# Attention value matmuls: three key tiles of four in two fp16 parts, and half of the mask made by GpSimd

## The chip, the cores and the metric

One core of one Trainium2 chip. The metric is the device time of one execution in microseconds, median of several runs; a profiled execution of the same kernel gives the trace.

## The reference, cut to what matters

Four layers run one after the other on 4096 nodes with 128 features: graph attention, a mixture of experts, a second graph layer, a second mixture. The change is in the first, and in the mask that the third reads:

```python
Qn = _cos_normalize(features @ Wq.T)
Kn = _cos_normalize(features @ Wk.T)
raw_att = Kn @ Qn.T
att = jnp.where(adj > 0, raw_att, NEG) * TEMP
att = jax.nn.softmax(att, axis=1)
prop_fea = att @ features
...
mask = (adj[:M] > 0) & valid[None, :]
```

`adj` is 4096 x 4096 int32, 64 MB. The scores are cosines, so the softmax needs no maximum: exp(score), times (adj > 0), summed over the keys.

## The kernel before, in words

`prepare` normalizes the rows, keeps them as values for attention and makes the queries' and keys' unit vectors, each as a high and a low fp16 part. It works in 8 groups of 512 nodes. Its `low_values` on GpSimd copies the fp32 values (L204) and subtracts the high fp16 part (L206), which ScalarE made in `high_values` (L283).

`attend` has 128 steps. Step k is (c, jp): c is one of 8 groups of 512 nodes that receive, jp one of 16 pairs of 128-row key tiles. All engines run their own unrolled list and meet by semaphores:

- SyncE loads 512 KB of adjacency (int32, 128 x 1024) into a ring of 4 buffers (L391). A buffer is free once the mask multiplication has read it.
- TensorE runs `scores(k + 2)`, six fp16 matmuls of 128x512 (L411), then `gather(k)`: the values times the probabilities, summed in one PSUM bank over the 16 pairs. The first key tile of a pair is one fp32 matmul (L423), the second is three fp16 ones: low values x high probabilities (L425), high x high (L426), high values x low probabilities (L428).
- ScalarE runs `exponentials(k + 1)` (L461), `keep_high(k)`, the copy of the second tile to fp16 (L469), and `keep_mask(k)`, the Sign of both tiles as uint8 (L472), which stays in SBUF for the third layer.
- VectorE runs `mask_exponentials(k + 1)` (L488: probs = (adj > 0) x probs), then `keep_low(k)` (L494: probs - p_hi), then, at jp 0, 3, 5 and 7, a piece of the `ending` of the previous group c: L507 copies the sums, L511 to L517 prepare, L524 adds, L532 measures.
- GpSimd has no work in this stage.

At jp 1 TensorE also turns the previous group's sums back (L437, four matmuls, eight records). The waits: L411 of k + 2 waits for the exponentials of k to have read their banks; L423 for the masked probabilities; L425 for p_hi, L428 for p_lo. The buffers p_hi and p_lo are two deep, probs four.

Of the kernel before, what the change touches and what calls it, by code (L numbers as in the profile page):

```python
# [7 lines left out]
F32 = mybir.dt.float32  # L8
# [9 lines left out]
P = 128  # L18
# [13 lines left out]
SLOTS = 2  # L32
LEVEL = 60.0
# [81 lines left out]
def prepare(nc, io, sb, ps):  # L115

    with ExitStack() as ctx:
# [18 lines left out]
        pairs = lambda ap: ap.rearrange("p (a b) d -> p a b d", b=2)  # L136
# [32 lines left out]
        with nc.Block() as block:  # L169
# [15 lines left out]
            @block.gpsimd  # L185
            def _(pool):
                nc.gpsimd.memset(sb["ident"][:, :], 0.0).then_inc(ident_ready, 1)
                pool.wait_ge(ident_ready, 1)
                nc.gpsimd.affine_select(out=sb["ident"][:, :], in_=sb["ident"][:, :], compare_op=ALU.not_equal,
                                        fill=1.0, base=0, pattern=[[-1, P]], channel_multiplier=1).then_inc(ident_ready, 1)  # L190
                nc.gpsimd.memset(v32[:, :, D - 1:D], V_SCALE).then_inc(ident_ready, 1)
                nc.gpsimd.memset(v16[:, :, 0, D - 1:D], V_SCALE).then_inc(ident_ready, 1)
                nc.gpsimd.memset(v16[:, :, 1, D - 1:D], 0.0).then_inc(ident_ready, 1)
                nc.gpsimd.memset(sb["turn"][:, :], 0.0).then_inc(ident_ready, 1)
                pool.wait_ge(ident_ready, 6)
                nc.gpsimd.tensor_copy(sb["turn"][:, 0:D - 1], sb["ident"][:, 0:D - 1]).then_inc(ident_ready, 1)
                nc.gpsimd.tensor_copy(sb["turn"][:, D:D + 1], sb["ident"][:, D - 1:D]).then_inc(ident_ready, 1)
                nc.gpsimd.tensor_scalar(sb["turn"][:, D - 1:D], sb["ident"][:, D - 1:D], 1.0, None, ALU.subtract)\
                    .then_inc(ident_ready, 1)

                def low_values(g, u):
                    pool.wait_ge(feat_ready, g + 1)
                    two = bass.ds(g * 2, 2)
                    nc.gpsimd.tensor_copy(v32[:, two, 0:D - 1], pairs(feat[:, u, :, :])[:, :, 0, 0:D - 1])  # L204
                    pool.wait_ge(v_hi_ready, RING + g + 1)
                    nc.gpsimd.tensor_tensor(v16[:, two, 1, 0:D - 1], pairs(feat[:, u, :, :])[:, :, 1, 0:D - 1],  # L206
                                            v16[:, two, 0, 0:D - 1], ALU.subtract).then_inc(v_lo_ready, 1)

                pipelined(pool, GROUPS, [(0, low_values)], slots=RING)
                pool.wait_ge(norms_ready, 1)  # L210
                pool.wait_ge(qk_copied, GROUPS)
                pipelined(pool, GROUPS, [(0, lambda g, u: scale_rows(pool, nc.gpsimd, g, u, 1))], slots=RING)
# [65 lines left out]
            def _(act):  # L278
                act.sem_inc(v_hi_ready, RING)
                act.sem_inc(qk_squared, SLOTS)  # L280
                def high_values(g, u):
                    act.wait_ge(feat_ready, g + 1)
                    nc.scalar.activation(v16[:, bass.ds(g * 2, 2), 0, 0:D - 1], pairs(feat[:, u, :, :])[:, :, 1, 0:D - 1],  # L283
                                         ACT.Copy).then_inc(v_hi_ready, 1)
# [60 lines left out]
def attend(nc, io, sb, ps):  # L345

    with ExitStack() as ctx:
        buf = lambda name, shape, dt=F32: ctx.enter_context(nc.sbuf_tensor(name, shape, dt))
        sem = lambda name: ctx.enter_context(nc.semaphore(name))
        LOADS = 4  # L350
# [6 lines left out]
        p_hi = buf("p_hi", [P, SLOTS, GROUP], F16)  # L357
        p_lo = buf("p_lo", [P, SLOTS, GROUP], F16)
# [4 lines left out]
        kT = sb["x1"][:, :, :].bitcast(F16)  # L363
        SUM_BANK, ROW_BANK = 4, 6
# [7 lines left out]
        mask_kept = sem("mask_kept")  # L372
        hi_ready = sem("hi_ready")
# [7 lines left out]
        with nc.Block() as block:  # L381

            @block.sync
            def _(sp):
                for k in range(STEPS):
                    c, jp = divmod(k, PAIRS)
                    u = k % LOADS
                    if k >= LOADS:

                        sp.wait_ge(masked, k - LOADS + 1)  # L390
                    sp.dma_start(adj[:, u, :], io["adj"][k:k + 1, :, :].rearrange("a p n -> (a p) n"))\  # L391
# [8 lines left out]
            def _(pe):  # L400
# [14 lines left out]
                def gather(k):  # L415
# [4 lines left out]
                    if jp == 0 and c >= 2:  # L420

                        pe.wait_ge(sums_copied, c - 1)
                    nc.tensor.matmul(out, v32[:, jp, :], probs[:, k % RING, 0:GROUP], start=(jp == 0), stop=False)  # L423
                    pe.wait_ge(hi_ready, k + 1)
                    nc.tensor.matmul(out, v16[:, jp, 1, :], p_hi[:, u, :], start=False, stop=False)  # L425
                    nc.tensor.matmul(out, v16[:, jp, 0, :], p_hi[:, u, :], start=False, stop=False)  # L426
                    pe.wait_ge(lo_ready, k + 1)
                    nc.tensor.matmul(out, v16[:, jp, 0, :], p_lo[:, u, :], start=False, stop=(jp == PAIRS - 1))\  # L428
                        .then_inc(pair_used, 1)
# [23 lines left out]
            def _(act):  # L453
# [10 lines left out]
                def keep_high(k):  # L464
# [4 lines left out]
                    nc.scalar.activation(p_hi[:, k % SLOTS, :], probs[:, k % RING, GROUP:], ACT.Copy).then_inc(hi_ready, 1)  # L469

                def keep_mask(k):
                    nc.scalar.activation(mask[:, k * W:(k + 1) * W], probs[:, k % RING, :], ACT.Sign).then_inc(mask_kept, 1)  # L472
# [7 lines left out]
                act.wait_ge(mask_kept, STEPS)  # L480

            @block.vector
            def _(dve):
# [8 lines left out]
                def keep_low(k):  # L492
                    dve.wait_ge(hi_ready, k + 1)
                    nc.vector.tensor_tensor(p_lo[:, k % SLOTS, :], probs[:, k % RING, GROUP:], p_hi[:, k % SLOTS, :], ALU.subtract)\  # L494
# [1062 lines left out]
def build(nc, io):  # L1557
    with ExitStack() as ctx:
# [5 lines left out]
        with ExitStack() as graph:  # L1564
            sb["mask"] = graph.enter_context(nc.sbuf_tensor("mask", [P, TILES * N], mybir.dt.uint8))
            with ExitStack() as attention:
                sb["v32"] = attention.enter_context(nc.sbuf_tensor("v32", [P, PAIRS, D], F32))
                sb["v16"] = attention.enter_context(nc.sbuf_tensor("v16", [P, PAIRS, 2, D], F16))
# [43 lines left out]
```

## Time and profile before

| | |
|---|---|
| median of 3 runs | 1033.2 us (1032.11 to 1036.44) |
| the profiled execution | 1035.4 us, span 1033.6 us |
| mean granted TensorE clock | 0.932 |
| PE busy | 888.2 us (86%) |
| DVE busy | 685.7 us (66%) |
| ACT busy | 583.1 us (56%) |
| POOL busy | 156.2 us (15%) |
| adjacency loads | 128 of 512 KB, median 3.8 us to landing |

PE is TensorE, DVE VectorE, ACT ScalarE, POOL GpSimd, SP SyncE; PEld is TensorE's weight load. L411 is line 411 of the kernel. The attention stage runs from about 69 to 444 us of the span. A busy PE row overlaps with its neighbours, since matmuls are pipelined: their pace is read from the starts.

### The profile page before, as it was taken

Reading aid. Unit: us, or ns where it says so; the run is one execution under the profiler, and the core shown is the slowest. Engines: PE = TensorE matmul, PEld = TensorE weight load, DVE = VectorE, ACT = ScalarE, POOL = GpSimd, SP = SyncE. Lnnn points to the kernel's source line nnn. Section 1 sums busy time; section 2 is a strip of 40 time slices with the busy share of each in tenths; the row PEclk is TensorE's granted clock in tenths of the full one; section 3 lists DMA queues with packets and bytes.
Section 4 is the critical chain, followed back from the end, with each engine's and each line's share of the span. In section 5 each row is a group of like instructions: output and inputs, shape, how many; then the busy total and the mean of one; then the engine's idle time right before and its main releaser. Section 6 shows DMA issues by size and latency. Waiting matters only on the chain. (4 is left out here: it accounts for less than half of the span.)

```text
span 1033.6 us, 14114 instructions
## 1 busy us (share of the span) xinstructions
PE 888.2 (86%) x4290; PEld 565.1 (55%) x4290; DVE 685.7 (66%) x1459; ACT 583.1 (56%) x764; POOL 156.2 (15%) x143
## 2 busy tenths in 40 slices
PE   3579999999999999933975459999479999999997
PEld 2444444444444444422964459999346666666654
DVE  6876677776767677673476446566666766677664
ACT  2559888888888888852551335555233333333332
POOL 2230000000000000015111040000133323333232
PEclk9979999999999999955996769999779999999999
DMA  4126565656656565300000000000300000000000
GB/s 127 41 101 219 188 203 174 215 183 204 200 188 203 184 205 182 122 6 25 1 0 4 0 1 1 1 0 0 82 1 1 11 10 11 0 10 10 10 2 19
DMA packets 39007, 81.29 MB, mean 79 GB/s; under 512 B 5032, under 2 KB 20016, under 8 KB 38960
## 3 DMA queue, kind: packets, MB, share of 16 engines
q1 hardware_dynamic: 38256, 80.39, 24.4%
q8 instruction: 23, 0.38, 0.1%
q10 hardware_dynamic: 704, 0.33, 0.1%
q14 instruction: 24, 0.20, 0.1%
HBM read 76.51 MB, written 4.19 MB: 78 GB/s over the span
## 5 line engine op out<-in xcount | busy, mean ns | idle before, releaser
L488 DVE SCALAR_TENSOR_TENSOR probs<-adj,probs 128x1024 f32<-128x1024 int32 x128 | 156.7, 1224 | 105.3 <-ACT probs L461 105.1
L411 PE MATMUL ps<-x,qT 128*128 128x512 f16 x768 | 188.8, 383 | 3.2 <-PEq L169 3.2
L1432 ACT ACTIVATE hT<-ps,b_all 128x512 f32<-128x512 f32 x128 | 88.1, 689 | 164.9 <-PE ps L1512 158.2
L461 ACT ACTIVATE probs<-ps 128x1024 f32<-128x1024 f32 x128 | 131.1, 1024 | 51.4 <-PE ps L411 51.4
L1062 PE MATMUL ps<-parts,edges 128*128 (+1 forms) x1024 | 127.2, 288 | 23.7 <-POOL parts L1116 18.6
L1062 PEld LDWEIGHTS ps<-parts,edges 128*128 128x128 f32 x1024 | 126.7, 194 | 24.1 <-issue 18.7
L472 ACT ACTIVATE mask<-probs 128x1024 uint8<-128x1024 f32 x128 | 134.0, 1047 | 0.0
L423 PE MATMUL ps<-probs,v 128*128 128x512 f32 x256 | 130.7, 592 | 0.0
L411 PEld LDWEIGHTS ps<-x,qT 128*128 128x128 f16 x768 | 75.6, 99 | 95.5 <-issue 6.7
L1314 POOL TENSOR_TENSOR hT_lo<-hT,hT_hi 128x512 fp32r<-128x512 f32 x64 | 86.3, 1349 | 184.2 <-DVE hT_hi L1381 184.2
L1044 ACT ACTIVATE edges<-mask 128x1024 fp32r x64 | 67.7, 1060 | 55.9 <-PE ps L1062 55.8
L494 DVE TENSOR_TENSOR p_lo<-probs,p_hi 128x512 f16<-128x512 f32 x128 | 87.5, 684 | 0.1
L1381 DVE CAST hT_hi<-hT 128x512 fp32r<-128x512 f32 x128 | 66.5, 542 | 30.1 <-ACT hT L1432 27.6
L1383 DVE TENSOR_TENSOR hT_lo<-hT,hT_hi 128x512 fp32r<-128x512 f32 x64 | 78.8, 1231 | 2.2
L469 ACT ACTIVATE p_hi<-probs 128x512 f16<-128x512 f32 x128 | 79.6, 622 | 0.0
L1042 DVE CAST edges<-mask 128x1024 fp32r (+1 forms) x64 | 45.3, 709 | 50.8 <-PE ps L1062 48.0
L632 POOL TENSOR_TENSOR x<-x,beta 128x512 f32 x8 | 9.8, 1267 | 401.9 <-DVE xn L659 401.9
L1520 PE MATMUL ps<-hT_lo,w_all_hi 128*128 128x512 f32 x128 | 56.3, 440 | 6.2 <-DVE hT_lo L1383 5.8
L1507 PE MATMUL ps<-xT_hi,w_all_lo 128*128 128x512 f32 x128 | 58.4, 456 | 0.0
L423 PEld LDWEIGHTS ps<-probs,v 128*128 128x128 f32 x256 | 48.1, 190 | 17.3
L1509 PE MATMUL ps<-xT_hi,w_all_hi 128*128 128x512 f32 x128 | 51.2, 400 | 0.0
L1508 PE MATMUL ps<-xT_lo,w_all_hi 128*128 128x512 f32 x128 | 51.1, 399 | 0.0
(226 smaller groups left out, 1273.6 us busy)
## 6 DMA issues: line engine op xcount, KB each, us to landing
adj<-in_adj SPq DMA_DIRECT2D x128, 512.0 KB, 3.8
mask<-in_x SPq DMA_DIRECT2D x4, 512.0 KB, 5.7
feat_spill<-mask SPq DMA_DIRECT2D x8, 256.0 KB, 2.0
x_feat<-in_x SPq DMA_DIRECT2D x8, 256.0 KB, 3.8
x_feat<-feat_spill SPq DMA_DIRECT2D x8, 256.0 KB, 4.0
out<-x SPq DMA_DIRECT2D x8, 256.0 KB, 2.3
w_all<-in_W1b SPq DMA_DIRECT2D x1, 1024.0 KB, 5.8
w_pair<-in_W1a ACTq DMA_DIRECT2D x1, 128.0 KB, 2.5
```

Source lines behind the costliest of these rows:

```text
L411: ins = nc.tensor.matmul(out, qT[:, q_half, j], kT[:, c, k_half * GROUP:(k_half + 1) * GROUP], start=(n == 0), stop=(n == 2))
L423: nc.tensor.matmul(out, v32[:, jp, :], probs[:, k % RING, 0:GROUP], start=(jp == 0), stop=False)
L461: nc.scalar.activation(probs[:, k % RING, :], ps[:, b:b + 2, :].rearrange("p b n -> p (b n)"), ACT.Exp, scale=1.0 / QK_SCALE ** 2).then_in ...
L469: nc.scalar.activation(p_hi[:, k % SLOTS, :], probs[:, k % RING, GROUP:], ACT.Copy).then_inc(hi_ready, 1)
L472: nc.scalar.activation(mask[:, k * W:(k + 1) * W], probs[:, k % RING, :], ACT.Sign).then_inc(mask_kept, 1)
L488: nc.vector.scalar_tensor_tensor(out=probs[:, k % RING, :], in0=adj[:, k % LOADS, :], scalar=0.0, in1=probs[:, k % RING, :], op0=ALU.is_gt ...
L494: nc.vector.tensor_tensor(p_lo[:, k % SLOTS, :], probs[:, k % RING, GROUP:], p_hi[:, k % SLOTS, :], ALU.subtract)\
L1044: ins = nc.scalar.activation(edges[:, u, :], source, ACT.Copy)
L1062: ins = nc.tensor.matmul(ps[:, 4 * cu + s, 0:K], edges[:, u, h * GROUP + s * P:h * GROUP + (s + 1) * P], rows, start=first and u == 0 and ...
L1314: nc.gpsimd.tensor_tensor(hT_lo[:, e % 2, 0, :], hT[:, e % 2, 0, :], hT_hi[:, e % 2, 0, :], ALU.subtract)\
L1383: nc.vector.tensor_tensor(hT_lo[:, e % 2, 1, :], hT[:, e % 2, 1, :], hT_hi[:, e % 2, 1, :], ALU.subtract)\
L1432: nc.scalar.activation(hT[:, e % 2, f, :], ps[:, UP_BANK + n % 4, :], ACT.Gelu, bias=b1[:, e, f:f + 1])\
```

## The change

The pair's split changes by the parity of the step (`split_tiles`): in an even step both key tiles are split into two fp16 parts (six fp16 value matmuls, no fp32 one), in an odd step one is split and the other stays fp32. So three tiles of every four are split, where it was two of four. The copy to p_hi and the subtraction to p_lo are 1024 wide in even steps and 512 in odd ones. In an odd step the fp32 tile is now the second of the pair. ScalarE's Sign makes the mask of the first tile only; GpSimd makes that of the second, straight from the adjacency. So the load of adjacency waits for GpSimd as well, and its ring has 3 buffers. In `prepare` the values are kept accordingly: one fp32 tile and three split ones of every four.

```diff
 SLOTS = 2
+SPLIT = 3
...
                 def low_values(g, u):
                     pool.wait_ge(feat_ready, g + 1)
-                    two = bass.ds(g * 2, 2)
-                    nc.gpsimd.tensor_copy(v32[:, two, 0:D - 1], pairs(feat[:, u, :, :])[:, :, 0, 0:D - 1])
+                    one = bass.ds(g, 1)
+                    nc.gpsimd.tensor_copy(v32[:, one, 0:D - 1], feat[:, u, SPLIT:SUB, 0:D - 1])
                     pool.wait_ge(v_hi_ready, RING + g + 1)
-                    nc.gpsimd.tensor_tensor(v16[:, two, 1, 0:D - 1], pairs(feat[:, u, :, :])[:, :, 1, 0:D - 1],
-                                            v16[:, two, 0, 0:D - 1], ALU.subtract).then_inc(v_lo_ready, 1)
+                    halves = v16[:, one, :, :, 0:D - 1].rearrange("p a t b d -> p (a t) b d")
+                    nc.gpsimd.tensor_tensor(halves[:, :, 1, :], feat[:, u, 0:SPLIT, 0:D - 1], halves[:, :, 0, :], ALU.subtract)\
+                        .then_inc(v_lo_ready, 1)
...
-                    nc.scalar.activation(v16[:, bass.ds(g * 2, 2), 0, 0:D - 1], pairs(feat[:, u, :, :])[:, :, 1, 0:D - 1],
-                                         ACT.Copy).then_inc(v_hi_ready, 1)
+                    nc.scalar.activation(v16[:, bass.ds(g, 1), :, 0, 0:D - 1].rearrange("p a t d -> p (a t) d"),
+                                         feat[:, u, 0:SPLIT, 0:D - 1], ACT.Copy).then_inc(v_hi_ready, 1)
...
-        LOADS = 4
+        LOADS = 3
...
-        p_hi = buf("p_hi", [P, SLOTS, GROUP], F16)
-        p_lo = buf("p_lo", [P, SLOTS, GROUP], F16)
+        p_hi = buf("p_hi", [P, SLOTS, W], F16)
+        p_lo = buf("p_lo", [P, SLOTS, W], F16)
...
+        split_tiles = lambda k: min(2, SPLIT - 2 * (k % 2))
...
                         sp.wait_ge(masked, k - LOADS + 1)
+                        sp.wait_ge(mask_kept_pool, k - LOADS + 1)
...
-                    nc.tensor.matmul(out, v32[:, jp, :], probs[:, k % RING, 0:GROUP], start=(jp == 0), stop=False)
+                    tiles = split_tiles(k)
+                    first = jp == 0
+                    if tiles == 1:
+                        nc.tensor.matmul(out, v32[:, jp // 2, :], probs[:, k % RING, GROUP:], start=False, stop=False)
+                    values = lambda h, part: v16[:, jp // 2, 2 * (jp % 2) + h, part, :]
                     pe.wait_ge(hi_ready, k + 1)
-                    nc.tensor.matmul(out, v16[:, jp, 1, :], p_hi[:, u, :], start=False, stop=False)
-                    nc.tensor.matmul(out, v16[:, jp, 0, :], p_hi[:, u, :], start=False, stop=False)
+                    for h in range(tiles):
+                        moving = p_hi[:, u, h * GROUP:(h + 1) * GROUP]
+                        nc.tensor.matmul(out, values(h, 1), moving, start=first and h == 0, stop=False)
+                        nc.tensor.matmul(out, values(h, 0), moving, start=False, stop=False)
                     pe.wait_ge(lo_ready, k + 1)
-                    nc.tensor.matmul(out, v16[:, jp, 0, :], p_lo[:, u, :], start=False, stop=(jp == PAIRS - 1))\
-                        .then_inc(pair_used, 1)
+                    for h in range(tiles):
+                        ins = nc.tensor.matmul(out, values(h, 0), p_lo[:, u, h * GROUP:(h + 1) * GROUP], start=False,
+                                               stop=(jp == PAIRS - 1 and h == tiles - 1))
+                    ins.then_inc(pair_used, 1)
...
-                    nc.scalar.activation(p_hi[:, k % SLOTS, :], probs[:, k % RING, GROUP:], ACT.Copy).then_inc(hi_ready, 1)
+                    n = GROUP * split_tiles(k)
+                    nc.scalar.activation(p_hi[:, k % SLOTS, 0:n], probs[:, k % RING, 0:n], ACT.Copy).then_inc(hi_ready, 1)
 
                 def keep_mask(k):
-                    nc.scalar.activation(mask[:, k * W:(k + 1) * W], probs[:, k % RING, :], ACT.Sign).then_inc(mask_kept, 1)
+                    nc.scalar.activation(mask[:, k * W:k * W + GROUP], probs[:, k % RING, 0:GROUP], ACT.Sign).then_inc(mask_kept, 1)
...
+            @block.gpsimd
+            def _(pool):
+                for k in range(STEPS):
+                    pool.wait_ge(adj_landed[k % LOADS], 16 * (k // LOADS + 1))
+                    nc.gpsimd.tensor_scalar(mask[:, k * W + GROUP:(k + 1) * W], adj[:, k % LOADS, GROUP:], 0.0, None, ALU.is_gt)\
+                        .then_inc(mask_kept_pool, 1)
+                pool.wait_ge(mask_kept_pool, STEPS)
...
                     dve.wait_ge(hi_ready, k + 1)
-                    nc.vector.tensor_tensor(p_lo[:, k % SLOTS, :], probs[:, k % RING, GROUP:], p_hi[:, k % SLOTS, :], ALU.subtract)\
+                    n = GROUP * split_tiles(k)
+                    nc.vector.tensor_tensor(p_lo[:, k % SLOTS, 0:n], probs[:, k % RING, 0:n], p_hi[:, k % SLOTS, 0:n], ALU.subtract)\
                         .then_inc(lo_ready, 1)
```

## Rows read from the trace of the kernel before

**Rows 1.** Windows, steady attention: us, then busy per engine, clock, DMA share, GB/s.
```profile
140.00:440.00 300.00, 298.52 (x1200) 137.25 (x1198) 216.33 (x325) 258.89 (x313) 0.00 (x0) 1.00 0.58 189
```

**Rows 2.** Groups by line from 130 to 430 us, with forms.
```profile
L488 DVE SCALAR_TENSOR_TENSOR probs<-adj,probs 128x1024 f32<-128x1024 int32 x105 | 128.6, 1224 | 79.7 <-ACT probs L461 79.4
L472 ACT ACTIVATE mask<-probs 128x1024 uint8<-128x1024 f32 x106 | 110.9, 1047 | 0.0
L494 DVE TENSOR_TENSOR p_lo<-probs,p_hi 128x512 f16<-128x512 f32 x106 | 72.4, 683 | 0.0
L469 ACT ACTIVATE p_hi<-probs 128x512 f16<-128x512 f32 x105 | 65.3, 622 | 0.0
```

**Rows 3.** Timeline: start and duration in us, engine, line; idle before in brackets.
```profile
252.34 1.02 PE L423 MATMUL ps<-probs,v 128*128 128x512 f32 x2
252.54 1.02 ACT L461 ACTIVATE probs<-ps 128x1024 f32<-128x1024 f32 x1 [0.31 <-PE ps L411]
253.67 1.23 DVE L488 SCALAR_TENSOR_TENSOR probs<-adj,probs 128x1024 f32<-128x1024 int32 x1 [0.97 <-ACT probs L461]
253.85 1.46 PE L411 MATMUL ps<-x,qT 128*128 128x512 f16 x6
254.81 0.68 DVE L494 TENSOR_TENSOR p_lo<-probs,p_hi 128x512 f16<-128x512 f32 x1
255.14 1.02 PE L423 MATMUL ps<-probs,v 128*128 128x512 f32 x2
256.00 0.38 PE L425 MATMUL ps<-p_hi,v 128*128 128x512 f16 x1
256.65 0.59 PE L411 MATMUL ps<-x,qT 128*128 128x512 f16 x2
...
258.21 0.68 DVE L507 COPY sumsT<-ps 128x512 f32<-128x512 f32 x1
303.92 0.68 DVE L507 COPY sumsT<-ps 128x512 f32<-128x512 f32 x1
```

**Rows 4.** Timeline at the first steps: a matmul that waited for the low part.
```profile
76.55 0.68 DVE L494 TENSOR_TENSOR p_lo<-probs,p_hi 128x512 f16<-128x512 f32 x1
77.29 0.39 PE L428 MATMUL ps<-p_lo,v 128*128 128x512 f16 x1 [0.46 <-DVE p_lo L494]
```

**Rows 5.** Timeline of DVE around two pieces of the ending.
```profile
269.20 1.22 DVE L488 SCALAR_TENSOR_TENSOR probs<-adj,probs 128x1024 f32<-128x1024 int32 x1
271.37 1.23 DVE L488 SCALAR_TENSOR_TENSOR probs<-adj,probs 128x1024 f32<-128x1024 int32 x1 [0.34 <-ACT probs L461]
274.36 1.21 DVE L488 SCALAR_TENSOR_TENSOR probs<-adj,probs 128x1024 f32<-128x1024 int32 x1
```

**Rows 6.** Groups of POOL over the whole span, with forms.
```profile
L204 POOL COPY v<-mask 128x254 f32 x8 | 3.3, 407 | 23.4 <-DVE mask L242 23.4
L196 POOL COPY turn<-ident 128x127 f32<-128x127 f32 x1 | 0.3, 290 | 0.1
L198 POOL TENSOR_SCALAR turn<-ident 128x1 f32<-128x1 f32 x1 | 0.3, 273 | 0.0
L1314 POOL TENSOR_TENSOR hT_lo<-hT,hT_hi 128x512 fp32r<-128x512 f32 x64 | 86.3, 1349 | 184.2 <-DVE hT_hi L1381 184.2
```

**Rows 7.** Timeline and durations (min/median/max) where POOL and DVE work together.
```profile
50.40 1.53 DVE L166 TENSOR_TENSOR mask<-mask,rnorm 128x512 f32<-128x512 f32 x1
51.35 1.49 POOL L166 TENSOR_TENSOR mask<-mask,rnorm 128x512 f32 x1
54.75 0.69 DVE L268 TENSOR_TENSOR qT<-ps,qT 128x512 f16<-128x512 f32 x1 [1.37 <-ACT x L301]
55.25 1.04 POOL L166 TENSOR_TENSOR mask<-mask,rnorm 128x512 f32 x1
L1383 DVE TENSOR_TENSOR hT_lo<-hT,hT_hi x64: 691/1646/1668, 761.9 to 1026.2; 128x512 fp32r<-128x512 f32 x64
```

**Rows 8.** The adjacency tile: time from issue to landing of its 128 loads.
```profile
DMA to landing us min/median/max: 3.1/3.8/7.2
```

More of the change, by code:

```diff
@@ L135, in prepare @@
         v32, v16 = sb["v32"], sb["v16"]
-        pairs = lambda ap: ap.rearrange("p (a b) d -> p a b d", b=2)
         x_in = [sem(f"x_in{i}") for i in range(4)]
@@ L191, in _ @@
                 nc.gpsimd.memset(v32[:, :, D - 1:D], V_SCALE).then_inc(ident_ready, 1)
-                nc.gpsimd.memset(v16[:, :, 0, D - 1:D], V_SCALE).then_inc(ident_ready, 1)
-                nc.gpsimd.memset(v16[:, :, 1, D - 1:D], 0.0).then_inc(ident_ready, 1)
+                nc.gpsimd.memset(v16[:, :, :, 0, D - 1:D], V_SCALE).then_inc(ident_ready, 1)
+                nc.gpsimd.memset(v16[:, :, :, 1, D - 1:D], 0.0).then_inc(ident_ready, 1)
                 nc.gpsimd.memset(sb["turn"][:, :], 0.0).then_inc(ident_ready, 1)
@@ L372, in attend @@
         mask_kept = sem("mask_kept")
+        mask_kept_pool = sem("mask_kept_pool")
         hi_ready = sem("hi_ready")
@@ L1566, in build @@
             with ExitStack() as attention:
-                sb["v32"] = attention.enter_context(nc.sbuf_tensor("v32", [P, PAIRS, D], F32))
-                sb["v16"] = attention.enter_context(nc.sbuf_tensor("v16", [P, PAIRS, 2, D], F16))
+                sb["v32"] = attention.enter_context(nc.sbuf_tensor("v32", [P, GROUPS, D], F32))
+                sb["v16"] = attention.enter_context(nc.sbuf_tensor("v16", [P, GROUPS, SPLIT, 2, D], F16))
                 sb["turn"] = attention.enter_context(nc.sbuf_tensor("turn", [P, D + 1], F32))
```

## The prediction

> **What bounds the kernel now.** I read first the page's table of engines, then the windows, to find which stage the change touches. It is the attention stage, some 375 of the 1033.6 us. Over its steady 300 us PE is busy for 298.5 us at a granted clock of 1.00, against 259 us on ACT, 216 on DVE and 0 on POOL [rows 1]: the stage is bound by TensorE, at its 2.4 GHz level. The groups by line give each operation's duration [rows 2]. Those of PE can't be summed, since matmuls overlap; the timeline has their spacing [rows 3]. Six fp16 score matmuls run from 253.85 to 255.14 us: 1.29, or 0.215 each. The fp32 one (two records) takes from 255.14 to 256.00, 0.86, which is four fp16 ones. Three fp16 value matmuls follow, 0.65. A step is 2.80 us (L411 at 253.85 and 256.65), with no gap. The eighth that shares a bank, 16 steps and one L437 group, is 45.7 us (L507 at 258.21 and 303.92, rows 3).
>
> Next, who is second? ACT waits only 0.31 us a step, DVE 0.97 us, both for scores [rows 3]. The DVE order is masked(k+1), low part(k), and then pieces of the ending. This order matters: the low part is the last input of a step's matmuls.
>
> **The change, term by term.** *PE.* An even step of the new kernel has 6 scores and 6 fp16 value matmuls: 12 x 0.215 = 2.59 us. An odd one has 6 + 3 + fp32 = 2.80 us as now. A pair of steps falls from 5.60 to 5.39, an eighth by 1.72 us, the stage by 13.8 us. That is the most that the change can give.
>
> *ACT.* Now 1.02 + 0.62 + 1.05 = 2.69 us a step. The copy to p_hi of an even step grows to 1024 wide, for which the nearest row is L472 at 1.05; the Sign halves, for which it is L469 at 0.62 [rows 2]. So 2.69 in an even step and 2.26 in an odd one: not above PE, no cost.
>
> *DVE.* The subtraction of an even step grows from 0.68 to 1024 wide; L488 has that size and two SBUF inputs, so 1.23 us [rows 2]. Busy time alone would go from 1.91 to 2.18 us a step plus the ending. But where is it in the chain? Count from the start of an odd step's fp32 matmul (252.34 in rows 3), when the scores of the step two ahead are done. Exp starts at +0.20, the mask multiplication at +1.33, the low part at +2.47; with 1.23 it ends at +3.70, and PE starts 0.06 behind a low part that it waited for (ended 77.23, matmul 77.29) [rows 4], so +3.76. PE itself wants it after 1.51 (odd gather) + 1.29 (scores) + 4 x 0.215 (high parts, no fp32 matmul ahead of them any more) = +3.66. So each even step stalls PE by 0.10, and a pair of steps takes 5.49 instead of 5.39. Before, the low part was ready about 0.9 us ahead. In the pair in which L437 runs PE is late anyway: 7 stalls, 0.70 us per eighth.
>
> *The ending.* Its pieces sit ahead of the odd steps' mask multiplications. They are hidden in DVE's idle time and in that 0.9 us of cover. The piece with L517 already starts the next L488 at 269.20, where the one behind it, at 271.37, puts the regular place at 271.37 - 2.80 = 268.57, 0.64 late; the one with L524 leads to 274.36 where 271.37 + 2.80 = 274.17, 0.19 late [rows 5]. With the cover gone both reach PE: 0.83 us per eighth.
>
> Sum without POOL: -1.72 + 0.70 + 0.83 = -0.19 per eighth, -1.5 us in all. Already nothing is left of the gain.
>
> *GpSimd.* 128 tensor_scalar of 128x512 int32 to uint8 on an engine that was idle here. No such row exists. One-input copies: 127 columns 290 ns, 254 columns 407 [rows 6], a slope of 0.92 ns a column; the tensor_scalar of 1 column takes 273. So 273 + 511 x 0.92 = 0.74 us. The bounds are 0.41 (the 254 copy) and 1.35 (the two-input 512, L1314). I take 0.74, being nearest to the one-input rows. The engine has time for it. It does not run beside DVE freely, though: in the stage before, GpSimd and DVE multiply 128x512 tiles that both lie in SBUF. With no such DVE work beside it GpSimd's takes 1.04 us, and DVE takes 0.68 for that size (L494, rows 2); together they take 1.49 and 1.53. DVE's L268, with a PSUM input, keeps its 0.69 beside the same GpSimd work [rows 7]. In the last stage L1383 goes from 691 ns to a median of 1646 with L1314 beside it [rows 7]. So two-SBUF-input work of DVE and GpSimd work take turns. L488 and L494 are both of this kind (adj and probs, probs and p_hi). The time for which DVE is held is shorter than the GpSimd record: L1383's extra 0.96 of a 1.39 record that began 0.29 earlier leaves 0.14 of the record free (estimate), so about 0.60 of 0.74.
>
> When does it strike? The GpSimd operation starts as its load lands; the load starts as the mask multiplication three steps before ends; landing takes 3.1 to 7.2, median 3.8 us [rows 8]. Call M the start of an odd step's L488. It ends at M + 1.23, its load lands at M + 5.03, the GpSimd operation holds the inputs from about M + 5.1 to M + 5.7. The next odd L488 is due at M + 5.49. It is 0.21 late, and that is in the chain with no cover. The other GpSimd operation of the pair is the even one: its L488 ends at M + 4.03, the load lands at M + 7.83, which is M' + 2.13 of the next pair, beside the wide low part (M' + 1.14 to 2.37). It holds DVE to M' + 2.97, where the even L488 is due at 2.80. That has slack: an odd step's low part would be ready at 2.47 + 0.68 + 0.06 = 3.21 and is wanted after 1.29 + 1.29 + 0.86 + 0.43 = 3.87. No cost. So a pair takes 5.70. Seven of these per eighth give 1.47. GpSimd's operations also meet L517 (two SBUF inputs): I put 0.4 per eighth, a choice between 0 and one whole hold of 0.60.
>
> The Trainium skill, page "SBUF — State Buffer", section "Who interferes with whom", says that a DVE instruction with two SBUF inputs contends with a GpSimd one that reads SBUF, and that the later one waits for the whole of the earlier. By that rule the trace agrees, apart from the 0.14 us; the hold would be 0.74, a pair 5.84 and the whole 8 us more than my sum. The third rival below is where the same taking of turns costs most.
>
> *Adj ring of 3, wait of SP on GpSimd.* The next user of a buffer starts three steps, some 8.3 us, behind the previous one, less 1.2 for its own work: 7.0 against a landing of 3.8 [rows 8]. GpSimd has finished long before DVE. Nothing else stands in SP's queue but the x_feat loads. No cost; a landing near 7.2 would cost one step some tenths.
>
> *Preparation.* GpSimd's subtraction grows by 127 columns, by 0.33 us at the pace of L1314 (1.35 for 512, rows 6, an estimate), its copy shrinks by 0.12 (407 to 290 ns), ACT's copy grows by a like amount. DVE idles for its scores there and all is off the chain; 0 to 2 us, I take 0.5.
>
> Sum: 8 x (-1.72 + 0.70 + 0.83 + 1.47 + 0.40) + 0.5 = 8 x 1.68 + 0.5 = +13.9 us. The profiled execution took 1035.4 us, 1.8 outside its span of 1033.6, and is 2.2 above the median of 1033.2. That makes 1049.3 in its terms and 1047.1 beside the median, 1047 for short.
>
> **The rivals.**
> - *PE's saving comes through* (faster). The mechanism is GpSimd work that falls into DVE's idle time each time, plus a low part on time. For: landing of 3.1 to 3.7 us would put the hold ahead of M + 5.49; the 0.10 stall is as small as my reading error. Against: the endings still cost 0.83. 8 x (-1.72 + 0.83) = -7 us: 1026, at best 1019 without the endings' cost. It decides at a hold that ends before M + 5.4.
> - *Everything cancels* (same). No extra wait by GpSimd but my stalls as computed: -1.5, some tenths more per pair make +4: 1032 to 1038.
> - *Each GpSimd operation hits the chain* (slower by more). Landing above 4.3 us, or a phase shifted by an ending, lets the operation meet the odd L488 or the low part behind it; then a pair takes 5.49 + 0.60 = 6.09: 7 pairs make 4.2: 8 x (-1.72 + 0.70 + 0.83 + 4.2 + 0.6) = +37 us: 1070. For: DVE is busy 216.3 / 300 of the stage [rows 1], 33.0 us of an eighth; with 8 x 0.55 of wider low parts and 16 holds of 0.60 that is 47.0 us of a forecast eighth of 47.4, with no room for bad placing. Against: part of the endings' DVE work (PSUM, one input) can run beside GpSimd.
> - *The GpSimd operation is slow*, 1.35 us: hold 1.2, so a pair takes 6.3, 0.81 over 5.49: 8 x (-0.19 + 7 x 0.81) = +44 us: 1077.
>
> The Trainium skill, page "GPSIMD Engine Reference", section 3.1, has a case of 512 elements on a tight loop at 769 ns. No run here shows it; by it the operation takes 0.77 and the sum rises by about 2 us.
>
> **How the numbers follow.** A difference below 0.5% (5 us) can't be told from no change here. Chances: forecast (1039 to 1058) 0.42; each operation hits or is slow (above 1058) 0.22; cancels 0.22; saving comes through 0.14. So slower 0.64, same 0.22, faster 0.14. Range: from 1027 to 1072, which leaves out the lower half of the faster rival and most of the slow operation; the likeliest case's own range is 1039 to 1058.
>
> **What would show it.** In the profile after: PE busy less than full in the attention stage, with waits of L4xx low-part matmuls for DVE p_lo of 0.1 to 0.4 us in even steps and none for ACT; the mask multiplication, constant at 1211 to 1226 ns now, with a tail up to 1.8 us, waiting behind POOL; a pair of steps of about 5.7 us, the eighth 47.4; the GpSimd operation near 0.74. The prediction is wrong if the eighth is below 45.7, if L488's duration stays at 1.23 (no contention), or if GpSimd takes over 1 us. If SP waits for POOL or the adjacency's landing is waited for, the ring of 3 was the fault that I left out.

## The result and the profile after

The changed kernel takes 1046.4 us (median of 4, 1043.05 to 1049.49) against 1034.8 for the kernel before on the same chip: a ratio of 1.0111, 95% interval 1.0066 to 1.0155. It is slower, by some 11.5 us or 1.1%; forecast were +13.9 us.

The stage of the change first: the same window as in [rows 1]. Behind the 300.00 us stand the busy time of PE, PEld, DVE, ACT and POOL, the granted clock, the DMA share and GB/s.

```profile
140.00:440.00 300.00, 287.56 (x1229) 126.29 (x1227) 253.44 (x318) 233.44 (x308) 179.30 (x102) 1.00 0.59 191
```

The clock is still 1.00, TensorE's 2.4 GHz level. TensorE, which had 298.5 us of work in 300, has 287.6; VectorE has gone from 216 to 253. So TensorE now waits, and for one thing, by the chain of waits from 130 to 430 us (who waited for whom: us in total, times, longest):

```profile
POOL mask L499 <- DMA adj<-in_adj: 120.9, 97, 2.5
ACT probs L473 <- PE ps L415: 67.5, 102, 2.4
DVE probs L509 <- ACT probs L473: 43.3, 63, 1.7
PEld ps L439 <- DVE p_lo L516: 34.2, 46, 2.3
...
PE ps L439 <- DVE p_lo L516: 13.7, 14, 1.9
```

The low-part matmuls (L439, L428 before) wait for the subtraction (L516). A wait of less than about 0.17 us doesn't show in the PE row, because the previous matmul's record (0.38 for a pace of 0.215) covers it; it shows in PEld, the weight load. VectorE does not wait for loads: the ring of 3 is no bottleneck. The durations, by line and form (out<-in, count, busy us, mean ns), to be held against [rows 2]:

```profile
L499 POOL TENSOR_SCALAR mask<-adj 128x512 uint8<-128x512 int32 x102 | 179.1, 1756 | 121.2 <-DMA adj<-in_adj 120.9
L509 DVE SCALAR_TENSOR_TENSOR probs<-adj,probs 128x1024 f32<-128x1024 int32 x103 | 129.8, 1260 | 45.3 <-ACT probs L473 43.3
L516 DVE TENSOR_TENSOR p_lo<-probs,p_hi 128x1024 f16<-128x1024 f32 x51 | 66.2, 1298 | 0.0
L482 ACT ACTIVATE p_hi<-probs 128x1024 f16<-128x1024 f32 x51 | 53.5, 1049 | 0.0
L516 DVE TENSOR_TENSOR p_lo<-probs,p_hi 128x512 f16<-128x512 f32 x51 | 41.0, 804 | 0.0
```

GpSimd's operation takes 1.76 us, not 0.74. Yet VectorE's rows are stretched by only 0.04, 0.08 and 0.12 us on the mean (against 1224, 1218 and 684 ns in experiment 1, which leaves GpSimd's operations out). The timeline around one ending shows how (VectorE and GpSimd, and the low-part matmuls):

```profile
264.91 1.49 POOL L499 TENSOR_SCALAR mask<-adj 128x512 uint8<-128x512 int32 x1 [0.84 <-DMA adj<-in_adj]
265.84 1.23 DVE L509 SCALAR_TENSOR_TENSOR probs<-adj,probs 128x1024 f32<-128x1024 int32 x1 [0.79 <-ACT probs L473]
...
270.53 1.58 POOL L499 TENSOR_SCALAR mask<-adj 128x512 uint8<-128x512 int32 x1 [0.98 <-DMA adj<-in_adj]
270.68 1.10 DVE L516 TENSOR_TENSOR p_lo<-probs,p_hi 128x512 f16<-128x512 f32 x1
...
272.26 1.11 DVE L539 SCALAR_TENSOR_TENSOR x_feat<-x_feat,keep 128x128 f32<-128x128 f32 x4
273.40 1.23 DVE L509 SCALAR_TENSOR_TENSOR probs<-adj,probs 128x1024 f32<-128x1024 int32 x1
...
274.03 1.95 POOL L499 TENSOR_SCALAR mask<-adj 128x512 uint8<-128x512 int32 x1 [1.92 <-DMA adj<-in_adj]
274.55 1.63 DVE L516 TENSOR_TENSOR p_lo<-probs,p_hi 128x1024 f16<-128x1024 f32 x1
...
276.23 0.60 PE L439 MATMUL ps<-p_lo,v 128*128 128x512 f16 x2 [1.61 <-DVE p_lo L516]
```

Read it from the bottom. TensorE stood 1.61 us because the wide subtraction ended late, at 276.18. It was stretched by 0.41 (1.63 for 1.22) by GpSimd, and it began late, since the L509 ahead of it stood behind the ending piece with L539; that piece in turn stood behind a narrow subtraction stretched from 0.68 to 1.10. The first two rows show the other case: GpSimd began 0.93 before L509, was still running, and L509 has its plain 1.23. So GpSimd keeps VectorE out only at the beginning of its 1.49 us, and two more pairs of rows of the profile after say for how long, and what happens the other way round:

```profile
216.22 1.49 POOL L499 TENSOR_SCALAR mask<-adj 128x512 uint8<-128x512 int32 x1 [1.97 <-DMA adj<-in_adj]
216.56 1.35 DVE L509 SCALAR_TENSOR_TENSOR probs<-adj,probs 128x1024 f32<-128x1024 int32 x1
...
280.45 1.22 DVE L516 TENSOR_TENSOR p_lo<-probs,p_hi 128x1024 f16<-128x1024 f32 x1
280.61 2.40 POOL L499 TENSOR_SCALAR mask<-adj 128x512 uint8<-128x512 int32 x1 [1.18 <-DMA adj<-in_adj]
```

An L509 that began 0.34 us behind GpSimd is only 0.12 longer than its 1.23, so VectorE was free some 0.46 us after GpSimd's start. A GpSimd operation that began 0.16 us behind the wide subtraction takes 2.40, 0.91 more than 1.49, while the subtraction had 1.06 to go: GpSimd waited for nearly the whole of it. So the two do take turns, but the shares differ. This text calls "hold" the time for which GpSimd keeps a VectorE instruction from its inputs, 0.41 to 0.44 us here where it strikes whole (L509 goes from 1.22 to 1.66 at most), and "cover" the time for which a low part is ready before TensorE wants it.

Over the six full eighths between the first and the seventh copy of the sums (L507 before, L529 after; 121.09 to 395.47, and 122.44 to 404.14 us) an eighth went from 45.73 to 46.95 us, +1.22 where 1.68 was forecast. The last copy is at 447.93 for 437.65: +10.3 us by the end of the stage. A "copy" is VectorE's copy of the sums, and "an eighth" stands for this mean over six.

### The profile page after: what moved, and what is told of

The parts are those of the page before. It is cut to its first block and busy times, and to the rows that moved or that the text cites. A ratio compares the mean times of both kernels' runs of the same rounds, so it can differ in the third digit from the quotient of the medians.

```text
span 1047.7 us, 14554 instructions
## 1 busy us (share of the span) xinstructions
PE 885.4 (85%) x4354; PEld 556.1 (53%) x4354; DVE 737.0 (70%) x1459; ACT 557.0 (53%) x764; POOL 380.8 (36%) x271
## 5 line engine op out<-in xcount | busy, mean ns | idle before, releaser
L499 POOL TENSOR_SCALAR mask<-adj 128x512 uint8<-128x512 int32 x128 | 223.7, 1749 | 157.7 <-DMA adj<-in_adj 157.5
L509 DVE SCALAR_TENSOR_TENSOR probs<-adj,probs 128x1024 f32<-128x1024 int32 x128 | 162.9, 1272 | 63.4 <-ACT probs L473 61.3
L473 ACT ACTIVATE probs<-ps 128x1024 f32<-128x1024 f32 x128 | 131.1, 1024 | 87.4 <-PE ps L415 87.4
L516 DVE TENSOR_TENSOR p_lo<-probs,p_hi 128x1024 f16<-128x1024 f32 (+1 forms) x128 | 133.5, 1043 | 0.0
L482 ACT ACTIVATE p_hi<-probs 128x1024 f16<-128x1024 f32 (+1 forms) x128 | 106.9, 835 | 0.1
L485 ACT ACTIVATE mask<-probs 128x512 uint8<-128x512 f32 x128 | 79.4, 620 | 0.0
L439 PE MATMUL ps<-p_lo,v 128*128 128x512 f16 x192 | 62.9, 382 | 15.9 <-DVE p_lo L516 15.8
L435 PE MATMUL ps<-p_hi,v 128*128 128x512 f16 x192 | 72.8, 379 | 1.5 <-ACT p_hi L482 1.5
L436 PE MATMUL ps<-p_hi,v 128*128 128x512 f16 x192 | 72.8, 379 | 0.0
L430 PE MATMUL ps<-probs,v 128*128 128x512 f32 x128 | 65.4, 592 | 0.0
## 6 DMA issues: line engine op xcount, KB each, us to landing
w_all<-in_W1b SPq DMA_DIRECT2D x1, 1024.0 KB, 5.9
```

Source lines behind the costliest of these rows:

```text
L473: nc.scalar.activation(probs[:, k % RING, :], ps[:, b:b + 2, :].rearrange("p b n -> p (b n)"), ACT.Exp, scale=1.0 / QK_SCALE ** 2).then_in ...
L482: nc.scalar.activation(p_hi[:, k % SLOTS, 0:n], probs[:, k % RING, 0:n], ACT.Copy).then_inc(hi_ready, 1)
L499: nc.gpsimd.tensor_scalar(mask[:, k * W + GROUP:(k + 1) * W], adj[:, k % LOADS, GROUP:], 0.0, None, ALU.is_gt)\
L509: nc.vector.scalar_tensor_tensor(out=probs[:, k % RING, :], in0=adj[:, k % LOADS, :], scalar=0.0, in1=probs[:, k % RING, :], op0=ALU.is_gt ...
L516: nc.vector.tensor_tensor(p_lo[:, k % SLOTS, 0:n], probs[:, k % RING, 0:n], p_hi[:, k % SLOTS, 0:n], ALU.subtract)\
```

## The experiments

Each ratio is to the kernel before, timed on the same chip, with its 95% interval. The eighth comes from the one profiled execution. A "plain pair" is an even and an odd step without a piece of the ending and without the matmuls that turn the sums back.

**1. Without GpSimd's operations.** The second half of the mask is left uncomputed: zeros are written over it once.

```diff
-                        sp.wait_ge(mask_kept_pool, k - LOADS + 1)
...
-                for k in range(STEPS):
-                    pool.wait_ge(adj_landed[k % LOADS], 16 * (k // LOADS + 1))
-                    nc.gpsimd.tensor_scalar(mask[:, k * W + GROUP:(k + 1) * W], adj[:, k % LOADS, GROUP:], 0.0, None, ALU.is_gt)\
-                        .then_inc(mask_kept_pool, 1)
-                pool.wait_ge(mask_kept_pool, STEPS)
+                halves = mask[:, :].bitcast(F32).rearrange("p (k h n) -> p k h n", h=2, n=GROUP // 4)
+                nc.gpsimd.memset(halves[:, :, 1, :], 0.0).then_inc(mask_kept_pool, 1)
+                pool.wait_ge(mask_kept_pool, 1)
```

> The changed kernel without GpSimd's 128 mask operations: one write of zeros over the second half of the mask at the start of the stage stands in their place (so the third layer reads a wrong mask), and SyncE waits for VectorE alone. ScalarE still makes half of the mask. Theory A (late low part and endings eat TensorE's saving, GpSimd's turns at the SBUF inputs cost the rest): 8 x (-1.72 + 0.70 + 0.83) = -1.5 us against the kernel before, ratio 0.995 to 1.002; an eighth of 16 steps 45.5 us, a plain pair of steps 5.48. Rival B (the split alone is the whole loss, GpSimd is innocent): an eighth stays at 46.7 and the ratio at 1.011. Rival C (GpSimd is the whole loss): an eighth near 44.0, ratio 0.987.

Measured: ratio 1.0002 (0.9987 to 1.0017); an eighth 45.57, five of its copies 45.50 to 45.51 apart (166.75, 212.25, 257.75, 303.25, 348.76). The split (with ScalarE's shorter Sign and the ring of 3) gives nothing by itself, and GpSimd's operations are the whole difference to the changed kernel. Here is a plain pair, and the stall that was forecast as 0.10:

```profile
274.72 1.22 DVE L513 TENSOR_TENSOR p_lo<-probs,p_hi 128x1024 f16<-128x1024 f32 x1
...
275.69 0.38 PE L435 MATMUL ps<-p_hi,v 128*128 128x512 f16 x1
275.99 0.11 PEld L438 LDWEIGHTS ps<-p_lo,v 128*128 128x128 f16 x2 [0.41 <-DVE p_lo L513]
275.99 0.61 PE L438 MATMUL ps<-p_lo,v 128*128 128x512 f16 x2
```

The fourth high-part matmul starts at 275.69, so the low part is wanted at 275.91; the subtraction ends at 275.94 and the matmul starts at 275.99, 0.08 late. The endings' loss is in the same trace, in one place:

```profile
221.44 1.11 DVE L536 SCALAR_TENSOR_TENSOR x_feat<-x_feat,keep 128x128 f32<-128x128 f32 x4
222.58 1.23 DVE L506 SCALAR_TENSOR_TENSOR probs<-adj,probs 128x1024 f32<-128x1024 int32 x1
223.73 1.22 DVE L513 TENSOR_TENSOR p_lo<-probs,p_hi 128x1024 f16<-128x1024 f32 x1
223.85 0.38 PE L435 MATMUL ps<-p_hi,v 128*128 128x512 f16 x1
225.00 0.60 PE L438 MATMUL ps<-p_lo,v 128*128 128x512 f16 x2 [0.77 <-DVE p_lo L513]
...
226.80 1.13 DVE L543 SCALAR_TENSOR_TENSOR x<-ps,denominator,x_feat 128x128 f32<-128x128 f32 x4
226.94 1.02 ACT L472 ACTIVATE probs<-ps 128x1024 f32<-128x1024 f32 x1 [1.47 <-PE ps L414]
228.07 1.22 DVE L506 SCALAR_TENSOR_TENSOR probs<-adj,probs 128x1024 f32<-128x1024 int32 x1
```

Behind the piece with L536 (L517 before) the low part is wanted at 223.85 + 0.215 = 224.07 and its matmul starts at 225.00: 0.93 late, 0.85 more than in a plain pair. The piece with L543 (L524 before) costs nothing: the L506 behind it starts 0.11 us after the exponentials' end (227.96), as it does in a plain pair.

**2. GpSimd's operations alone.** The kernel before, its split kept, with half of the mask made by GpSimd and a ring of 3.

```diff
-        LOADS = 4
+        LOADS = 3
...
+        mask_kept_pool = sem("mask_kept_pool")
...
                         sp.wait_ge(masked, k - LOADS + 1)
+                        sp.wait_ge(mask_kept_pool, k - LOADS + 1)
...
-                    nc.scalar.activation(mask[:, k * W:(k + 1) * W], probs[:, k % RING, :], ACT.Sign).then_inc(mask_kept, 1)
+                    nc.scalar.activation(mask[:, k * W:k * W + GROUP], probs[:, k % RING, 0:GROUP], ACT.Sign).then_inc(mask_kept, 1)
...
+            @block.gpsimd
+            def _(pool):
+                for k in range(STEPS):
+                    pool.wait_ge(adj_landed[k % LOADS], 16 * (k // LOADS + 1))
+                    nc.gpsimd.tensor_scalar(mask[:, k * W + GROUP:(k + 1) * W], adj[:, k % LOADS, GROUP:], 0.0, None, ALU.is_gt)\
+                        .then_inc(mask_kept_pool, 1)
+                pool.wait_ge(mask_kept_pool, STEPS)
```

> The kernel before with the other half of the change alone: GpSimd makes the second half of the mask, ScalarE the first, ring of 3 buffers, the split stays one tile of two. Theory A: the low part keeps its 0.9 us of cover, so VectorE's rows grow by up to 0.43 us when GpSimd is beside them, but TensorE waits at most in the steps of the endings: 0 to +3 us, ratio 0.998 to 1.003, an eighth 45.7 to 46.0. Rival C (GpSimd's operations alone are the loss, whatever the split): about +10 us, ratio 1.01.

Measured: ratio 1.0053 (1.0034 to 1.0072), an eighth 46.40. A miss for both: +5.5 us by the ratio, more than my 0 to 3 and half of the rival's 10. So the 0.9 us of cover is not enough in the endings:

```profile
174.58 1.10 DVE L504 TENSOR_TENSOR p_lo<-probs,p_hi 128x512 f16<-128x512 f32 x1
...
176.16 1.11 DVE L527 SCALAR_TENSOR_TENSOR x_feat<-x_feat,keep 128x128 f32<-128x128 f32 x4
177.30 1.23 DVE L498 SCALAR_TENSOR_TENSOR probs<-adj,probs 128x1024 f32<-128x1024 int32 x1
...
178.44 1.10 DVE L504 TENSOR_TENSOR p_lo<-probs,p_hi 128x512 f16<-128x512 f32 x1
...
179.60 0.39 PE L430 MATMUL ps<-p_lo,v 128*128 128x512 f16 x1 [0.43 <-DVE p_lo L504]
```

Two holds of 0.42 on top of the piece's 0.64 make 1.48, more than the 0.9 of cover, and TensorE waits for some 0.6 us: 0.43 in the row and 0.17 under the previous record. Only the pair behind this piece is longer than before, in each of the six eighths; the other pairs keep their old length (5.60, or 6.50 where the sums are turned back), though 27 of the 96 subtractions in the six eighths are stretched to about 1.10.

**3. A ring of 4 again.** p_hi and p_lo are packed to make room, and their indices follow.

```diff
-        LOADS = 3
+        LOADS = 4
...
-        p_hi = buf("p_hi", [P, SLOTS, W], F16)
-        p_lo = buf("p_lo", [P, SLOTS, W], F16)
+        p_hi = buf("p_hi", [P, SLOTS * W - GROUP], F16)
+        p_lo = buf("p_lo", [P, SLOTS * W - GROUP], F16)
```

> The changed kernel with 4 adjacency buffers again (p_hi and p_lo packed to 1536 columns to make room). Theory A: the ring costs nothing, since VectorE hardly waits for a load; the phase at which GpSimd works shifts, so an eighth 46.2 to 47.0, ratio 1.005 to 1.013. Rival D (the ring of 3 with SyncE waiting for GpSimd, 21 us in 17 waits, is what costs): an eighth 45.5, ratio 0.998.

Measured: ratio 1.0117 (1.0097 to 1.0138), an eighth 47.10, 0.1 above what I expected and far from the rival's 45.5. The ring costs nothing.

**4. The low part later on TensorE.** `gather_low` holds the low-part matmuls, cut from `gather`.

```diff
...
                         scores(k + SLOTS)
+                    if k:
+                        gather_low(k - 1)
                     if c and jp == TURN_STEP:
                         turn_back(c - 1)
                     gather(k)
+                gather_low(STEPS - 1)
                 turn_back(GROUPS - 1)
```

> The changed kernel with one order changed on TensorE: the low-part matmuls of step k are issued after the scores of step k + 3, ahead of the high-part matmuls of step k + 1, so that the low part has 1.29 us more. All results are made. Theory A (the low part is the last input of the step): the waits of the low-part matmuls vanish but for a few steps of the endings, an eighth 44.0 to 44.5, the whole -10 to -14 us, ratio 0.987 to 0.990. Rival E (VectorE with GpSimd's turns is out of time, 47 us of work per eighth as I reckoned with a hold of 0.60): an eighth stays above 46, ratio above 1.005; with the hold of 0.43 that the trace after shows that would be 37.4 + 16 x 0.43 = 44.3, just at the bound.

Measured: 1025.1 us, ratio 0.9908 (0.9886 to 0.9931), an eighth 44.53; both lie just outside what I expected (0.990, 44.5), and far from the rival's 1.005 and 46. By the two ratios the kernel is 2% faster than the changed one, with the same GpSimd work, and it is faster than the kernel before. Its waits from 130 to 430 us:

```profile
DVE probs L518 <- ACT probs L482: 19.3, 34, 1.5
...
PEld ps L445 <- DVE p_lo L525: 7.5, 15, 1.0
...
PE ps L445 <- DVE p_lo L525: 1.5, 4, 0.5
DVE probs L518 <- DMA adj<-in_adj: 0.5, 1, 0.5
```

TensorE's 13.7 us of waiting for the low part are 1.5, and VectorE's idle time, 43.3 before its mask multiplication, is down to 19.3: VectorE has the time, its results were only wanted too early. GpSimd pays for it where VectorE works without a pause. The longest GpSimd operation:

```profile
143.59 5.84 POOL L508 TENSOR_SCALAR mask<-adj 128x512 uint8<-128x512 int32 x1 [1.00 <-DMA adj<-in_adj]
```

VectorE ran five of its two-input instructions back to back from 142.85 to 148.07; GpSimd's operation ended 1.36 us after that, at 149.43.

**5. The low part later, without GpSimd's operations** (the edits of 1 and 4; half of the mask is left uncomputed).

> The late low part together with no GpSimd mask operations (zeros written once over the second half of the mask, which is left uncomputed). Theory A: nothing is left that delays TensorE, an eighth is the 43.99 us of its own matmuls, 0.5 below the late low part with GpSimd, the whole -13.8 us, ratio 0.985 to 0.989. Rival (TensorE's saving can't be had whole, VectorE or ScalarE is the next bound): an eighth stays near 44.5.

Measured: ratio 0.9882 (0.9866 to 0.9897), an eighth 44.02, the copies 44.02 apart each time. That is TensorE's own time, 1.71 under the 45.73 of before; 1.72 was the term. The whole is -12 us, where I expected -13.8. GpSimd still costs 0.5 per eighth beside the late low part.

**6. GpSimd writes, but reads nothing** (half of the mask is left uncomputed).

```diff
-                    nc.gpsimd.tensor_scalar(mask[:, k * W + GROUP:(k + 1) * W], adj[:, k % LOADS, GROUP:], 0.0, None, ALU.is_gt)\
+                    nc.gpsimd.memset(mask[:, k * W + GROUP:(k + 1) * W], 0)\
```

> The changed kernel in which GpSimd's 128 operations write zeros over the second half of the mask and read nothing (that half is left uncomputed); waits and semaphores stay. Theory A (GpSimd delays VectorE by its reads of SBUF, 0.43 us an operation): VectorE's rows are those without GpSimd, 1224, 684 and 1218 ns, an eighth 45.5, ratio 0.998 to 1.002. Rival F (any work of GpSimd delays VectorE, or the waits between the engines do): rows stretched, an eighth above 46, ratio above 1.005.

Measured: ratio 1.0005 (0.9995 to 1.0014), an eighth 45.61. The groups by line:

```profile
L509 DVE SCALAR_TENSOR_TENSOR probs<-adj,probs 128x1024 f32<-128x1024 int32 x106 | 129.8, 1224 | 52.0 <-ACT probs L473 50.6
L516 DVE TENSOR_TENSOR p_lo<-probs,p_hi 128x1024 f16<-128x1024 f32 x53 | 64.5, 1218 | 0.0
L499 POOL MEMSET mask<- 128x512 uint8 x105 | 55.2, 525 | 246.3 <-DMA adj<-in_adj 246.3
...
L516 DVE TENSOR_TENSOR p_lo<-probs,p_hi 128x512 f16<-128x512 f32 x52 | 35.5, 683 | 0.0
```

128 GpSimd operations with all their waits, and VectorE's rows are as without them. The waits and the writes cost nothing. The write is also shorter (0.53 for 1.76 us), so experiment 6 by itself can't tell GpSimd's reading from its computing. The rows of the profile after narrow it down: the hold ends about 0.46 us after the start of an operation that takes 1.49, so the later two thirds of its work hold nothing. That the first third holds VectorE because it reads fits both, but no run separates it.

**7. The ending's pieces in even steps, without GpSimd's operations** (half of the mask is left uncomputed).

```diff
-                    return {0: copy_sums, 3: add_features, 5: add_sums, 7: measure}
+                    return {0: copy_sums, 4: add_features, 6: add_sums, 8: measure}
```

> The changed kernel without GpSimd's mask operations (second half of the mask left uncomputed, as in the first run of the series) and with the pieces of VectorE's ending at steps 0, 4, 6 and 8 in place of 0, 3, 5 and 7. Theory A: there they sit ahead of the even steps' mask multiplication, which has 0.44 us of idle time and some 0.66 us of slack, so of the 0.83 us that the endings cost most goes: an eighth 44.7 to 44.9 in place of 45.5, ratio 0.993 to 0.996. Rival G (the parity is nothing, what counts is VectorE's total work): an eighth 45.5 as before.

Measured: ratio 0.9968 (0.9956 to 0.9981), an eighth 44.99. Half a microsecond per eighth is gone; the expected 44.7 to 44.9 is missed by 0.1, the ratio is just outside its window. The rest is one step: the narrow subtraction behind the same piece ends 0.4 us too late for its matmul, more than the slack that I gave it.

**8. The same move with GpSimd, all results made.**

> The changed kernel, all results made, with the same move of the ending's pieces to steps 0, 4, 6 and 8. Theory A: the endings' 0.83 us go as without GpSimd, its turns stay: an eighth 45.6 to 46.1 in place of 46.7, ratio 1.000 to 1.006. Rival G: no change, ratio 1.011.

Measured: ratio 1.0071 (1.0049 to 1.0092), an eighth 46.49 for 46.95. A gain of the same 0.5 per eighth, from a place 0.4 above the one that I expected; the ratio is 0.001 above my window. By the groups the narrow subtraction grew to 0.90 us on the mean (0.80 in the changed kernel): the moved pieces shift the phase, and the turns fall elsewhere.

**9. Both orders changed, all results made** (the edits of 4 and 7).

> The changed kernel, all results made, with both orders changed: low-part matmuls behind the next scores, and the ending's pieces at steps 0, 4, 6 and 8. The late low part alone left 0.5 us per eighth above TensorE's own 43.99. Theory A: the cover of 1.29 us already takes most of the endings, so 0 to 0.5 us per eighth more: -9.5 to -13.5 us against before, ratio 0.987 to 0.991. Rival H (the rest is GpSimd's turns, which the parity doesn't touch, or the pieces now meet more of them): as the late low part alone, 0.991, or worse.

Measured: 1024.0 us (1019.73 to 1024.75), ratio 0.9897 (0.9877 to 0.9917), an eighth 44.04, the 43.99 of TensorE's own work but for 0.05. The times don't tell it from experiment 4 (0.9908, 0.9886 to 0.9931); the 0.49 per eighth is read from one profiled execution of each. Here is a pair, the low part behind the scores:

```profile
257.00 1.46 PE L415 MATMUL ps<-x,qT 128*128 128x512 f16 x6
...
257.74 2.08 POOL L508 TENSOR_SCALAR mask<-adj 128x512 uint8<-128x512 int32 x1 [0.69 <-DMA adj<-in_adj]
258.30 0.59 PE L445 MATMUL ps<-p_lo,v 128*128 128x512 f16 x2
258.39 1.10 DVE L525 TENSOR_TENSOR p_lo<-probs,p_hi 128x512 f16<-128x512 f32 x1
258.73 1.02 PE L430 MATMUL ps<-probs,v 128*128 128x512 f32 x2
```

The subtraction is again stretched from 0.68 to 1.10, and no matmul waits.

**10. The late low part with a ring of 4, all results made** (the edits of 3 and 4).

> The changed kernel, all results made, with the late low part and 4 adjacency buffers. In the late kernel the steps are shorter and the GpSimd operation takes nearly 2 us, so SyncE's wait for it could now bite. Theory A (the ring is not the limit, VectorE waited once for a load): as the late low part alone, ratio 0.989 to 0.993. Rival D (the ring of 3 is what leaves the 0.5 us): an eighth 44.0, ratio 0.987.

Measured: ratio 0.9902 (0.9876 to 0.9927), an eighth 44.37, as the theory had it and 0.4 above the rival. SyncE waits for GpSimd often in experiment 4 (74 us in 54 waits) and hardly more than a microsecond of it arrives: 0.16 us per eighth, which the times can't tell.

## Why the prediction was right

The time (+11.5 for +13.9 us) and the mechanism were right: TensorE's saving is eaten by waits for the low part, by an ending that has lost its cover, and by the turns that GpSimd and VectorE take. Three terms of an eighth hold to 0.1 us. The two for GpSimd's turns, 1.87 together, measured 1.38, and they got there by errors that pull in opposite directions, which was luck. One of the prediction's own signs of being wrong, a GpSimd operation of over 1 us, did come.

- **TensorE's saving, 1.72 per eighth.** Right: 45.73 - 44.02 = 1.71 where nothing delays it (experiment 5).
- **The low part late by 0.10 in seven pairs, 0.70.** Right: a plain pair takes 5.48 where the matmuls need 5.39, the stall is 0.08 to 0.09, 0.6 per eighth. Experiment 4 shows the cause: later use, no stall.
- **The endings, 0.83.** Right in size: 45.50 - 44.02 - 0.63 = 0.85. The two pieces were not: the one with L517 costs all of the 0.85 (0.64 forecast), the one with L524 nothing (0.19 forecast), by the rows in experiment 1. The move to even steps takes back 0.51 (experiment 7), not most of it.
- **GpSimd's operation, 0.74 us.** Wrong by a factor of two: 1.48 at least, 1.64 in the median. The slope of 0.92 ns a column was that of fp32 copies; this one compares int32 and writes uint8, and which of these makes it slow no run tells. It fell on no chain, though: experiments 6 and 3 show that its waits and its writes cost nothing, and nobody but SyncE waits for it.
- **The hold of 0.60, seven times 0.21, and 0.40 at L517.** Wrong in size and place, near in the sum: 1.87 forecast, 46.95 - 45.57 = 1.38 measured. I had the hold as the operation less 0.14; for the real 1.48 us that would have been 1.34, about the rival with a slow operation and its +44 us. But the hold is some 0.42, for a narrow VectorE instruction as for a wide one (1.10 - 0.68, 1.63 - 1.22). The table gives the mean length of each pair in six eighths, from the starts of the even steps' exponentials (these run up to two steps ahead, so what the piece at jp 3 costs shows in the column of jp 6).

| pair at jp | 0 | 2 | 4 | 6 | 8 | 10 | 12 | 14 |
|---|---|---|---|---|---|---|---|---|
| before | 5.60 | 6.50 | 5.60 | 5.62 | 5.60 | 5.60 | 5.60 | 5.60 |
| experiment 2, GpSimd alone | 5.60 | 6.50 | 5.60 | 6.23 | 5.60 | 5.60 | 5.60 | 5.60 |
| experiment 1, split alone | 5.48 | 6.37 | 5.39 | 6.39 | 5.49 | 5.48 | 5.48 | 5.48 |
| the changed kernel | 5.57 | 6.45 | 5.41 | 7.21 | 5.49 | 5.48 | 5.55 | 5.76 |

Against experiment 1 the changed kernel loses 0.82 at the piece with L517, where two holds meet the missing cover, and 0.54 spread over other pairs, most of it in the last two of an eighth. It is not the 0.21 in each pair that was forecast: most plain pairs keep their 5.48. Landing took 3.3 us in the median, not 3.8, so that in those pairs the hold falls into VectorE's idle time ahead of an odd L509 (as at 264.91 and 265.84 above), or on an odd step's narrow subtraction, which has slack (it is 1.10 long at jp 11 in all six eighths, and the pair keeps its 5.48).

- **The ring of 3, nothing.** Right (experiments 3 and 10).
- **The preparation, 0.5 us in all.** Not shown: TensorE's first scores start at 69.06 us for 68.99, but the other runs have them anywhere from 67.9 to 69.5.
- **The page rule**, that the later of the two waits for the whole of the earlier. The measured part first: a two-input VectorE instruction and a GpSimd one that reads SBUF contend, and one that only writes does not (experiment 6). A GpSimd operation that came second waited for 0.91 of VectorE's remaining 1.06 us; a VectorE instruction that came second was held until 0.46 us after the start of an operation of 1.49. The rule stands in "SBUF — State Buffer" of the Trainium skill, section "Who interferes with whom". On which instructions contend the runs agree with it; on the whole of the earlier they agree, but for 0.15 us, where GpSimd comes second, and differ where VectorE does. The measurement decides. The other page that I cited, with 769 ns for 512 elements ("GPSIMD Engine Reference" of the Trainium skill, section 3.1), speaks of a tight loop at its best; this operation takes 1.48 us.

Of the rivals, the one in which TensorE's saving comes through needed no luck with the phase, as I had it, but another order: a low part that is wanted 1.29 us later. "Each GpSimd operation hits the chain" was refuted by the pairs of 5.48. "The GpSimd operation is slow" had the length right, and the hold that it was to bring wrong.

Why the same GpSimd work costs 1.38 us per eighth with the new split but 0.67 (46.40 - 45.73) with the old one can be read from the table: with the old one it costs 0.61 at the one piece and nothing in the other pairs, since the 0.9 us of cover takes single holds (the rest of the 0.67 is a shift of the copies themselves). What stays open is why the holds fall as they do: the last pairs of an eighth are hit and the middle ones not, and the phases weren't varied by themselves. Of the profiled span's +14.1, the 3.8 us behind the +10.3 at the stage's end are not the change's: in experiment 3, with the same work behind attention, that part takes 595.7 us, as it did before (1033.6 - 437.65 = 595.9), against 599.8 in this one execution, the longest of the four.

## What to carry to other kernels

When a change shortens the bound engine's step, look for the input that it needs last and count how long it was ready beforehand: here the fp32 matmul that was removed was the cover of the low part and of the endings. That cover can be won back by the order of issue alone: moving a step's one or two low-part matmuls behind the next scores turned +1.1% into -0.9%. And work given to an idle GpSimd was not free here, where VectorE reads two tiles from SBUF; cost it as the time for which it holds VectorE, in the steps where VectorE is late already.

## What the runs showed of the hardware that was not expected

- A GpSimd tensor_scalar of 128x512 from int32 to uint8 takes 1.48 us at least, against 0.41 for an fp32 copy of 254 columns and 0.53 for a uint8 memset of 512. Where it starts while VectorE is in a two-input instruction it first waits for its end, once through five of them in a row: up to 2.57 us in the changed kernel, 5.84 in experiment 4.
- It holds a VectorE instruction with two SBUF inputs for 0.42 us, at most 0.44, and 0.46 us after its own start it holds it no more. The memset holds none.
- The median landing of an adjacency load differs with the kernel and no rule was found: 3.8 us before, 3.3 in the changed kernel, 4.1 in experiment 1 and 3.4 in experiment 5, both of these without GpSimd's reading.
